# Turning the rotated q and k parts: 32 SBUF-to-SBUF transposing DMAs a block in place of 32 TensorE transposes and 4 ScalarE copies

## The reference: one transformer layer with attention and feed-forward side by side

```python
xn = layernorm(x)                        # x: 4 sequences x 2048 tokens x 256
q, k, v = split(xn @ w_qkv.T)            # 16 heads of 16
q, k = rope(q), rope(k)                  # x * cos + rot * sin
attn = softmax(q @ k.T * 16 ** -0.5)
out_attn = (attn @ v) @ w_out.T
out_ffn = (silu(xn @ wg.T) * (xn @ wu.T)) @ wd.T      # hidden 768, weights int / 127
out = x + out_attn + out_ffn
```

## Time and profile before

| | us |
|---|---|
| median of 3 runs | 2998.14 (2996.81 to 2999.5) |
| the profiled execution, its own time | 2996.64 |
| its span in the profile | 2994.9 |
| TensorE busy | 2883.3 (96%) |
| VectorE busy | 2693.8 (90%) |
| ScalarE busy | 2464.0 (82%) |
| GpSimd busy | 477.7 (16%) |

### The profile page before, as it was taken

How to read it: one execution, slowest core, us unless ns; L and a number is a source line. 1 busy time by engine, 2 the same in 40 slices (tenths; PEclk the granted TensorE clock), 3 DMA queues, 4 the chain that set the end, 5 groups by cost and what they waited for, 6 DMA issues and landing times.

```text
span 2994.9 us, 67199 instructions
## 1 busy us (share of the span) xinstructions
PE 2883.3 (96%) x27416; PEld 1052.8 (35%) x27416; DVE 2693.8 (90%) x2974; ACT 2464.0 (82%) x4609; POOL 477.7 (16%) x896
## 2 busy tenths in 40 slices
PE   5999996999999999999999999999999999999999
PEld 3666653233333333333333333333333333333336
DVE  6667667999999999999999999999999999999952
ACT  4544552899999999999999999999999999999972
POOL 4666662000000000000000000000000000000000
PEclk9999997999999999999999999999999999999999
DMA  3223331111111111111111111111111111111115
GB/s 109 88 95 114 97 96 47 27 31 31 31 31 31 31 31 31 31 31 31 31 31 31 31 31 31 31 31 30 31 31 31 31 31 31 31 31 31 31 62 177
DMA packets 124600, 137.14 MB, mean 46 GB/s; under 512 B 43264, under 2 KB 103296, under 8 KB 124288
## 3 DMA queue, kind: packets, MB, share of 16 engines
q1 hardware_dynamic: 124288, 132.79, 16.4%
HBM read 88.15 MB, written 34.08 MB: 41 GB/s over the span
## 4 chain that ended last, share of the span: by engine, by line
PE 85%; ACT 8%; DVE 4%; issue 3%; DMA 0%; POOL 0%; ACTq 0%; SPq 0%; DVEq 0%; POOLq 0%
PE psum L722 36%; PE psum L682 20%; PE psum L740 16%; ACT probs L885 5%; PE psum L592 5%; PE psum L564 4%; PE psum L665 2%; DVE row_max L1280 1%; PE psum L607 1%; ACT hT L797 1%; DVE stats L1048 1%; ACT stabT L877 1%; DVE xnT L1072 1%; DVE h L1200 0%; PE psum L701 0%
## 5 line engine op out<-in xcount | busy, mean ns | idle before, releaser
L1280 DVE TENSOR_REDUCE row_max<-psum 128x1 f32<-128x1024 f32 x2048 | 2335.6, 1213 | 51.8 <-PE psum L682 51.6
L885 ACT ACTIVATE probs<-psum 128x512 f32<-128x512 f32 x4096 | 2178.2, 597 | 193.2 <-PE psum L740 94.4
L722 PE MATMUL psum<-probs,v_op 128*32 128x256 f32 (+1 forms) x15872 | 1296.0, 398 | 0.0
L740 PE MATMUL psum<-q_op,k_op 51*128 51x512 f16 x4096 | 863.7, 381 | 31.7 <-ACT probs L885 23.7
L682 PE MATMUL psum<-k_op,q_op 48*128 48x512 f16 x4096 | 806.5, 391 | 24.7 <-DVE row_max L1280 20.5
L682 PEld LDWEIGHTS psum<-k_op,q_op 48*128 48x128 f16 x4096 | 196.1, 92 | 894.8 <-issue 528.7
L722 PEld LDWEIGHTS psum<-probs,v_op 128*32 128x32 f32 x15872 | 312.4, 108 | 526.6 <-issue 497.7
L740 PEld LDWEIGHTS psum<-q_op,k_op 51*128 51x128 f16 x4096 | 371.1, 94 | 274.7 <-ACT probs L885 73.1
L1033 POOL TENSOR_TENSOR acc_sb<-acc_sb,inv_rows 128x512 f32<-128x512 f32 x64 | 81.7, 1277 | 1911.0 <-DMA inv_rows<-inv_dram 1911.0
L592 PE MATMUL psum<-xnT,wf 128*128 128x512 f16 x768 | 178.8, 379 | 0.0
L804 ACT ACTIVATE parts<-qk_rot 128x512 f16<-128x512 f32 x64 | 40.1, 627 | 147.9 <-POOL qk_rot L963 147.9
(11 more groups left out here) (102 smaller groups left out, 954.4 us busy)
## 6 DMA issues: line engine op xcount, KB each, us to landing
qk_dram<-staged SPq DMA_DIRECT2D x64, 256.0 KB, 4.8
q_op<-qk_dram SPq DMA_DIRECT2D x128, 128.0 KB
k_op<-qk_dram SPq DMA_DIRECT2D x128, 128.0 KB
x_ln<-in_x SPq DMA_DIRECT2D x16, 512.0 KB, 4.4
x_res<-in_x SPq DMA_DIRECT2D x16, 512.0 KB, 5.4
y_dram<-y_blk SPq DMA_DIRECT2D x16, 512.0 KB, 3.2
k_op<-qk_dram SPq DMA_DIRECT2D x128, 64.0 KB
q_op<-qk_dram SPq DMA_DIRECT2D x128, 64.0 KB
```

Source lines behind the costliest of these rows:

```text
L722: mm = pe.matmul(bank(7)[32 * j:32 * j + 32, n0:n1], v_op[:, h % 2, t, :], probs[:, g3 % PROBS, j * BANK + n0:j * BANK + n1], start=(t == ...
L740: pe.matmul(bank(b), k_op[r:e, h % SLOTS, t * P:(t + 1) * P], q_op[r:e, h % SLOTS, j * BANK:(j + 1) * BANK], start=True, stop=True).then_i ...
L885: nc.scalar.activation(probs[:, g2 % PROBS, j * BANK:(j + 1) * BANK], bank(b), ACT.Exp, scale=to_score).then_inc(s2_used, 1)
L1280: nc.vector.tensor_reduce(row_max[:, hl % 2, t, half:half + 1], psum[:, 2 * half * BANK:(2 * half + 2) * BANK], AX.X, ALU.max).then_inc(s1 ...
```

## The change

The eight squares of a tile are turned by eight DMAs on SP's queue, from `parts` straight to `staged` (`transpose=True`), 32 in a block and 512 in all. TensorE's transposes of `parts` and ScalarE's copies `stage` are gone, with their two semaphores and the waits on them. A new semaphore `parts_turned` counts the DMAs. SP waits for it before it writes `staged` out, and ScalarE waits for it in `hi_part` before it writes `parts` again. SP waits for `staged_out` before it turns into `staged` again.

```diff
@@ SP, block_a(k, left)
             if left >= 2:
                 load_x(k + 2)
 
-            sp.wait_ge(partsT_saved, BLK * (k + 1))
+            if k > 0:
+                sp.wait_ge(staged_out, 16 * N_STAGED * k)
+            for t in range(BLK):
+                sp.wait_ge(parts_ready, BLK * k + t + 1)
+                for a in range(PARTS):
+                    for qg in range(2 * KT):
+                        sp.dma_start(staged[:, a, qg, t * P:(t + 1) * P], parts[:, t, a, qg * P:(qg + 1) * P],
+                                     transpose=True).then_inc(parts_turned, 16)
+            sp.wait_ge(parts_turned, 16 * N_TURNED * (k + 1))
@@ TensorE, turn_x(k, first)
-            if not first:
-                pe.wait_ge(partsT_saved, BLK * k)
@@ TensorE, block_a, behind pair j
-                if 1 <= j <= BLK:
-
-                    t = j - 1
-                    pe.wait_ge(parts_ready, BLK * k + t + 1)
-                    if t < 2:
-                        pe.wait_ge(xT_saved, KT * (k + 1))
-                        pe.wait_ge(xlo_ready, KT * (k + 1))
-                    else:
-                        pe.wait_ge(partsT_saved, BLK * k + t - 1)
-                    turned = bank(t % 2).bitcast(F16)
-                    for n in range(PARTS * 2 * KT):
-                        a, qg = divmod(n, 2 * KT)
-                        mm = pe.transpose(turned[:, n * P:(n + 1) * P], parts[:, t, a, qg * P:(qg + 1) * P], identh[:, :])
-                    mm.then_inc(partsT_full, 1)
@@ ScalarE, hi_part(k, t)
             act.wait_ge(qk_ready, BLK * k + t + 1)
             if not (isinstance(k, int) and k == 0):
-                act.wait_ge(partsT_full, BLK * k)
+                act.wait_ge(parts_turned, 16 * N_TURNED * k)
@@ ScalarE, block_a(k, last)
-            def stage(t):
-
-                if t == 0 and k > 0:
-                    act.wait_ge(staged_out, 16 * N_STAGED * k)
-                act.wait_ge(partsT_full, BLK * k + t + 1)
-                nc.scalar.activation(staged[:, :, :, t * P:(t + 1) * P],
-                                     bank(t % 2).bitcast(F16).rearrange("p (a q n) -> p a q n", a=PARTS, q=2 * KT),
-                                     ACT.Copy).then_inc(partsT_saved, 1)
```

More of the change, by code:

```diff
@@ L107, in layer_program @@
     N_STAGED = 2 * KT
+    N_TURNED = BLK * PARTS * 2 * KT
     ident = sb(keep, "ident", [P, P])
@@ L257, in layer_program @@
     parts_ready = sem("parts_ready")
-    partsT_full = sem("partsT_full")
-    partsT_saved = sem("partsT_saved")
+    parts_turned = sem("parts_turned")
     staged_out = sem("staged_out")
@@ L650, in _ @@
         pe.wait_ge(y_ready, BLK * NBLK)
-        pe.wait_ge(partsT_saved, BLK * NBLK)
         def project(q):
@@ L826, in block_a @@
             gate(1)
-            stage(0)
             h_hi(k, 0)
@@ L830, in block_a @@
             gate(2)
-            stage(1)
             h_hi(k, 1)
             gate(3)
-            stage(2)
             h_hi(k, 2)
             gate(4)
-            stage(3)
             h_hi(k, 3)
```

## The result

| | before | changed | ratio |
|---|---|---|---|
| median, us | 2997.72 | 3424.09 | 1.1422 (1.1402 to 1.1442) |
| span of the profiled execution, us | 2994.9 | 3424.2 | |
| TensorE's mean granted clock | 0.991 | 0.929 | |

The kernel became 14.2% slower, 426 us. The direction and the place were forecast, the size was not: 151 us were. (The profiled execution of the changed kernel is the longest of its four, whose times lie between 3422.80 and 3425.96 us.)

What follows compares the result with a forecast made beforehand. TensorE was taken to bound the kernel before, SP's DMA issues after: 10.7 us a block, 14 times, gives +150, block 14 +1, so 2996.64 + 151 = 3148, forecast 3150 us at the median. Range 3010 to 3650.

Steps and rivals of the forecast that it cites:

- X = 0.785: SP's time in us from one transposing DMA issue to the next, taken from plain stabT issues; 31 X = 24.3 us.
- The bound from above, 1.84 us: Upper limit for SP's issue step: the slowest issue in a run of ten, waiting behind those before it.
- backing up: Rival: SP's issues wait for transfers, step 1.2 to 1.84 us; 3645 us at 1.84; chance 0.17.
- The loop: Stage A, one round a block: hi_part to xn_ready, load of x, 31 X, landing; 38.2 us, 10.7 over 27.5.
- Its first term: From hi_part(k, 0) to xn_ready: a chain of short pieces, 11.5 us, where it took 14.65 before.
- The landing: Last DMA of a block's 32: lands 2.0 us after its issue, as SBUF-to-SBUF DMAs do.
- Block 14: No wait for xn_ready: DMAs start 1.8 us after hi_part, end at 28.1, against about 27; +1 us.
- SP's other work costs nothing: SP's writes and loads after the last DMA, some 6 us, fit before the next xn_ready 11.5 us away.
- Turned at the rate of plain DMAs: Rival: SP issues transposing DMAs as fast as plain ones, 0.507 us plus 0.05 between; 3045 us; chance 0.13.
- The clock falls: Rival: TensorE's clock drops in stage A's loop; costs nothing unless the mean is under 0.64; nothing added, no chance given.
- What remains of a block, if nothing new binds, is 25.7 us: Stage A block: 27.5 us less TensorE's 1.8 us of transposes, all taken to be on the chain.
- Hidden, and faster: Rival: issue step under 0.38 us keeps the DMAs within the block, TensorE gives back 28.8 us; 2968 us; chance 0.09.

Runs made afterwards that it cites:

- e1_alone: Small separate program, not the layer: SP and ScalarE queues issue turning and plain DMAs, VectorE scales alone and beside GpSimd; turning issue 1.09 us after a landing, 1.23 in a row.
- e2_plain: Changed kernel with its 32 DMAs a block as plain copies, squares not turned; 3117.61 us, ratio 1.0403.
- e3_half: Changed kernel with only the high parts turned, 16 DMAs a block, low parts of staged set to zero; 3116.22 us, ratio 1.0395.
- e4_early: Changed kernel with SP's load of x and wait for xn_ready moved behind the eight DMAs of tile 0; 3315.3 us, ratio 1.1058.
- e5_wide: Changed kernel with a tile's eight squares turned by one DMA, 4 DMAs a block; 3000.33 us, ratio 1.001.
- e7_wide_act: e5_wide with normalise for blocks 2 to 15 moved from VectorE to ScalarE; 2967.53 us, ratio 0.9899.
- e8_before_act: Kernel before the change, with TensorE's transposes and ScalarE's copies, and normalise moved from VectorE to ScalarE; 2995.51 us, ratio 0.9993.
- e6_wide8: Changed kernel with two DMAs of four squares for each tile, 8 DMAs a block; 2998.97 us, ratio 1.0005.

## Why the prediction was wrong

**The step that failed is "so I take X = 0.785".** A transposing DMA costs SP 1.27 us from one to the next, 1.30 with the occasional long one. With the mean X of the 14 rounds the error is 31 x (1.305 - 0.785) = 16.1 us a round, 14 rounds: 225 us, and 16 more in block 14. The rows that I took for near, SBUF-to-SBUF issues of 0.75 to 0.77 us, were of plain DMAs, and e1_alone and e2_plain show that turning doubles the issue of the very same square. The bound from above, 1.84 us, was wide enough, and the measured time lies in the range. But that was luck: I gave this X a chance of 0.17 under the name "backing up", for a cause that the runs refute.

**The loop was right.** Its form, hi_part(k, 0) to xn_ready, load of x, 31 X, landing, gives with measured terms 12.78 + 0.47 (331.82 to 344.60 to 345.07) + 40.4 + 2.5 = 56.2 us, the measured round. e3_half changes its number of DMAs, e4_early its first term; their times came 10 and 2 us from what the loop gives. e5_wide, with 4 DMAs, takes the loop off the path; its time was 30 us off and is the subject of the last point.

**Its first term was 1.3 us too small,** 12.78 instead of 11.5, 18 us over 14 rounds. The chain was summed with 2.22 us for `normalise`; in the changed kernel it runs beside three of GpSimd's subtractions and takes 3.93. The rest of the chain was 0.4 us shorter than its sum. **The landing** was 2.4 instead of 2.0 us and ScalarE starts 0.1 later: 7 us. With X that makes 17.9 of the 18.0 us by which a round was missed.

**Block 14** was predicted at +1 and measured at +24.5. Besides X, SP was not free when its first parts were ready: it first issued the writes of `staged` and `y`, the load of `x_res` and the loads for stage B, and began at 843.53, 5.6 us after `hi_part` and not 1.8. Its run of 32 also has an issue of 4.27 us and took 2.7 us more than the 40.4 above. "SP's other work costs nothing" was right for blocks with the wait for `xn_ready` and wrong for the one without it.

**The rivals.** "Turned at the rate of plain DMAs" fell: SP pays 1.27 us instead of 0.65 for a square, and plain DMAs at 32 a block gave 3118 us, not 3045, so plain DMAs of squares were priced too low as well. The Trainium skill ("Advanced Engine Details and Errata", section "X-Bar Transpose (TRN2)") states that transposing DMAs are as fast as regular ones. The issue times disagree; of the transfer alone it may hold, since landings are 2.4 and 1.9 us after the start of an issue of 1.23 and 0.60 us. (That rival's own terms add up to 3048 us, not to the 3045 in the prediction.)

"The queue backs up" fell: with a wait for each landing the issue still takes 1.09 us, and the last of 32 land as soon as the others.

"The clock falls": it did, to 0.79 in the round shown and 0.76 over stage A, with TensorE busy for 26.7 of 56.2 us. From `hi_part(k, 0)` to the load of x, at 331.82 and 387.39 in this kernel and at 300.09 in e2_plain:

```profile
331.82:344.60 12.78, 7.23 (x24) 2.62 (x24) 6.88 (x9) 7.36 (x13) 11.61 (x10) 0.76 0.52 165
387.39:400.17 12.78, 8.30 (x24) 2.91 (x24) 6.88 (x9) 7.46 (x13) 11.61 (x10) 0.67 0.52 165
300.09:312.87 12.78, 6.83 (x24) 2.52 (x24) 6.88 (x9) 7.36 (x13) 11.61 (x10) 0.87 0.57 180
```

The windows run from the one start to the other, and the three stretches are equally long at clocks of 0.76, 0.67 and 0.87. Rounds 1 to 13 are each 14.5 us longer than their run of 32 issues, at mean clocks from 0.74 to 0.78. So the clock costs nothing in this loop, as the sum had it.

**"What remains of a block, if nothing new binds, is 25.7 us"** was wrong in a way that the slow kernel hides. With the DMAs out of the way, e5_wide gives 27.44 us. I had read from the chain that TensorE's 0.45 us x 4 were on the path, which they were, and had not asked what VectorE would meet when the pairs moved up by 1.8 us. "Hidden, and faster" would have been 3000 us, no gain; the 2968 us that I gave it came only with e7_wide_act, 2967.5 us, and that the two agree is in part luck. A block there is shorter than 25.7 us, since moving `normalise` gives 0.3 us by itself (27.22 in e8_before_act for 27.50), and its block 0 is 1.55 us longer than before (27.10 for 25.55). The two runs e7 and e8 show that both edits are needed: the pairs must be shorter and `normalise` must not stand in VectorE's queue beside GpSimd's work. How much of the 33 us is due to the stretch of 1 us and how much to VectorE's queue being free of the other 2.2 us, they don't tell apart.

## What to carry to other kernels

A DMA has a price on the queue that issues it, apart from bandwidth and landing; if many of them end a wait, count issues first, and look for one DMA that covers the same squares. Where a kind of instruction is in no row, the nearest row of another kind can be far off: the short program that measures it would have settled some 240 of the 275 us that I was off.

When work leaves the engine that bounds a loop, the others move against each other: look in the timeline for pairs that will now run side by side before counting the gain.

## What the runs showed of the hardware

- A transposing DMA of float16 costs its issuing queue 1.09 to 1.23 us on SP and 1.18 to 1.27 on ScalarE (e1_alone). On SP this holds for 16 rows of 128 up to eight squares of 128 x 128 at once, which land 2.2 to 3.0 us after their issue. In the kernels the medians are 1.23 us for one square (changed kernel), 1.27 for four (e6_wide8) and 1.31 for eight (e5_wide); single issues take up to 4.5 us (e4_early) and single landings up to 7.7, and no run shows why. A plain copy of a square has a median of 0.60 us (e2_plain).
- VectorE's scale of 128 x 256 float32 from SBUF to SBUF takes 0.41 us alone and 1.30 us beside a running GpSimd operation of 1.26 us (e1_alone), as if they took turns.
